# Two-layer recurrent and routed-expert kernel: steps split into parts, a new order of the steps, and fewer pauses on GpSimd

## The reference

```
xn = layernorm(x); x = x + mixer0(xn) * silu(experts0(xn))
xn = layernorm(x); x = x + mixer1(xn) * silu(experts1(xn))

mixer0: xx = shift(xn) - xn; m = tanh((xn + xx*maa_x) @ w1) @ w2      # five token mixes: w, k, v, r, g
        r, k, v, g = from xn + xx*(maa + m); w = decay + tanh(xw @ dw1) @ dw2
        y_t = r_t (S + u k_t v_t);  S = exp(-exp(w_t)) S + k_t v_t     # 2 heads of 64
        out = (groupnorm(y) * silu(g)) @ Wo
experts0: top 2 of 8 by xn @ Wg, softmax of the two; each (silu(x W1) * (x W2)) W3, hidden 256
mixer1: softmax attention, 16 heads of key size 8, over the 512 tokens of a batch
experts1: top 2 of 8, the input of each scaled by a sigmoid gate, plus one shared expert, hidden 256
```

## Time and profile before

| | |
|---|---|
| median of 3 runs (lowest to highest) | 2901.74 us (2898.67 to 2910.47) |
| the profiled execution, its own time | 2902.1 us |
| its span | 2900.3 us, mean granted TensorE clock 0.951 |
| TensorE busy (PE) | 2514.9 us, 87% |
| weight loads (PEld) | 1770.9 us, 61% |
| VectorE busy | 1731.5 us, 60% |
| ScalarE busy | 1411.9 us, 49% |
| GpSimd busy | 1328.8 us, 46% |
| indirect gathers on GpSimd | 256 of 0.99 us, 253.7 us |
| pauses on GpSimd | 192 of 1.68 us, 322.5 us |
| chain that ended last | PE 52%, issue 18%, POOL 15%, ACT 7%, DVE 7% |

### The profile page before, as it was taken

One profiled execution on the slowest core, in us unless ns is written; L12 is line 12 of the kernel. 1 busy time (PEld: TensorE's weight loads), 2 busy tenths in 40 slices (PEclk: granted clock), 3 DMA queues, 4 the chain that ended last, 5 costly groups with the idle time before them and its releaser, 6 DMA issues.

```text
span 2900.3 us, 54969 instructions
## 1 busy us (share of the span) xinstructions
PE 2514.9 (87%) x18122; PEld 1770.9 (61%) x18122; DVE 1731.5 (60%) x4229; ACT 1411.9 (49%) x2613; POOL 1328.8 (46%) x1332
## 2 busy tenths in 40 slices
PE   5678888988889898898989888898898989989887
PEld 2556666666666666566666666666666666666644
DVE  3355657566565755656566565655656666565653
ACT  1234554554545454455545455454454545455545
POOL 2545353555535255443544535355443534535211
PEclk6779999999999999999999999999999999999989
DMA  4233334334333333423334333333424334333222
GB/s 121 69 118 99 114 97 119 114 110 126 96 110 108 112 108 109 125 87 114 113 103 122 94 115 102 118 106 110 125 83 120 116 93 123 100 115 97 79 64 70
DMA packets 384822, 306.26 MB, mean 106 GB/s; under 512 B 37440, under 2 KB 376096, under 8 KB 384544
## 3 DMA queue, kind: packets, MB, share of 16 engines
q1 hardware_dynamic: 368160, 269.16, 31.4%
q0 software_dynamic: 16384, 33.59, 4.0%
HBM read 247.15 MB, written 54.39 MB: 104 GB/s over the span
## 4 chain that ended last, share of the span: by engine, by line
PE 52%; issue 18%; POOL 15%; ACT 7%; DVE 7%; DMA 1%; SPq 0%; another core or an unknown queue 0%; POOLq 0%; ACTq 0%; DVEq 0%
PE bank_st L846 6%; PE bank_s L831 6%; PE bank_y L691 5%; PE bank_g L672 5%; PE bank_pv L860 5%; PE bank_h L672 5%; POOL yg L1137 4%; POOL pause_sb L1061 3%; DVE rowmax L1374 2%; PE bank_mix L702 2%; ACT probs L1010 2%; PE bank_mix L743 2%; ACT ks L995 2%; DVE xn L1245 1%; PE bank_mix L765 1%
## 5 line engine op out<-in xcount | busy, mean ns | idle before, releaser
L1374 DVE TENSOR_REDUCE rowmax<-bank_s 128x1 f32<-128x512 f32 x1016 | 699.2, 688 | 446.1 <-PE bank_s L831 388.6
L1010 ACT ACTIVATE probs<-bank_st 128x512 f32<-128x512 f32 x992 | 589.5, 594 | 373.9 <-PE bank_st L846 350.3
L831 PE MATMUL bank_s<-ks,qs 128*128 128x512 f32 x1016 | 451.5, 444 | 122.1 <-DVE rowmax L1374 118.6
L846 PE MATMUL bank_st<-qs,ks 128*128 128x512 f32 x992 | 501.3, 505 | 47.2 <-ACT probs L1010 45.0
L1061 POOL TENSOR_TENSOR pause_sb<-ones_sb,power_sb 128x8 f32<-128x8 f32 x192 | 322.5, 1680 | 197.4 <-DMA ys_d<-y_sb 102.5
L831 PEld LDWEIGHTS bank_s<-ks,qs 128*128 128x128 f32 x1016 | 196.7, 194 | 219.5 <-DVE rowmax L1374 138.6
L846 PEld LDWEIGHTS bank_st<-qs,ks 128*128 128x128 f32 x992 | 190.7, 192 | 168.1 <-ACT probs L1010 107.9
L691 PEld LDWEIGHTS bank_y<-wbuf,hid 128*128 128x128 f32 x1920 | 254.2, 197 | 60.3 <-DVE hid L1268 26.8
L672 PEld LDWEIGHTS bank_h<-xT_sb,wbuf 128*128 128x128 f32 x1920 | 253.7, 195 | 57.0 <-issue 25.4
L672 PEld LDWEIGHTS bank_g<-xT_sb,wbuf 128*128 128x128 f32 x1920 | 260.9, 199 | 41.8 <-issue 23.3
L672 PE MATMUL bank_h<-xT_sb,wbuf 128*128 128x128 f32 x1920 | 267.4, 282 | 18.0 <-DVE th L1256 17.3
(11 more groups left out here) (244 smaller groups left out, 3874.3 us busy)
## 6 DMA issues: line engine op xcount, KB each, us to landing
wbuf<-up SPq DMA_DIRECT2D x480, 128.0 KB
wbuf<-gate SPq DMA_DIRECT2D x480, 128.0 KB
wbuf<-down SPq DMA_DIRECT2D x480, 128.0 KB
xs_sb<-xs_d SPq DMA_DIRECT2D x96, 256.0 KB
ys_d<-y_sb SPq DMA_DIRECT2D x96, 256.0 KB, 2.5
xs_sb<-xs_d SPq DMA_DIRECT2D x32, 192.0 KB
ys_d<-y_sb SPq DMA_DIRECT2D x32, 192.0 KB, 2.6
x_next<-x SPq DMA_DIRECT2D x16, 256.0 KB, 3.2
```

The lines of the kernel that those rows point to most:

```text
L831: mm(room(s, b)[:], qs[:, slot, q * P:(q + 1) * P], ks[:, slot, j, :], start=True, stop=True).then_inc(filled[b], 1)
L846: mm(room(s, b)[:], ks[:, slot, j, k * P:(k + 1) * P], qs[:, slot, :], start=True, stop=True).then_inc(filled[b], 1)
L1010: A(probs[:, turn % PRING, h % HG, :], ps[:], ACT.Exp).then_inc(emptied[b], 1)
L1374: v.reduce_max(rowmax[:, h // HG % 2, NT * (h % HG) + q:NT * (h % HG) + q + 1], content(s, b)[:], AX).then_inc(emptied[b], 1)
```

## The change

Four steps become several, each with a due time of its own, so that other steps of the same engine can stand between the parts:

- `norm` keeps the moments and `vareps`; the wait for `rstd` and the four `xn` are `normx`.
- `route` keeps the top two; the gates (a softmax or a sigmoid of the two scores, `wtmp`) are `weigh`.
- `rank` keeps the first four of the 15 instructions of `places`; `place` 1, 2 and 3 have the rest.
- `wkv` keeps the group norm's moments and `gvar`; the two `yn` instructions and the wait for GpSimd's power are `yn`.
- the four `ks` copies of `stack` are four steps `keys`, 0.76 us of the plan apart; the wait for a free slot is a function of its own.

No instruction of these is added or removed. The pause of `rest()` stays only ahead of the fourth and seventh DMA of each group of eight, 8 a batch.

All constants of the plan are set anew, and so are the offsets in `LATER` for all five engines. In GpSimd's order the offsets of the kinds that the text below speaks of go from 0.26 to 0.22 (`norm`), 0.28 to 0.28 (`gather`), -0.54 to -0.54 (`decays`), 0.48 to 0.34 (`scatter`); in VectorE's `norm` has -0.06 and `normx` 0.42. The diff without the long `LATER` tables and without the bodies that only move into another branch:

```diff
-PERIOD = 167.91
-MIX_START = 0.91
+PERIOD = 167.87
+MIX_START = 0.94
 MIX_EVERY = 5.92
-DECAYS_BEFORE = 5.86
-CROSS_BEFORE = 5.77
-FINISH_AFTER = 4.27
+DECAYS_BEFORE = 7.76
+CROSS_BEFORE = 3.72
+FINISH_AFTER = 4.9
...
-WEIGHTS_BEFORE = 17.22
-GATHER_AFTER = 8.11
-COMBINE_AFTER = 29.52
-YOUT_AFTER = -0.18
-NORM0_AT = 100.17
+WEIGHTS_BEFORE = 23.74
+GATHER_AFTER = 7.68
+COMBINE_AFTER = 25.79
+YOUT_AFTER = -0.21
+NORM0_AT = 100.28
...
-RANK_AFTER = 4.58
-SCATTER_AFTER = 1.7
-FETCH_AFTER = 7.18
+RANK_AFTER = 4.29
+SCATTER_AFTER = 21.46
+FETCH_AFTER = 1.99
...
-SCATTER_EVERY = 3.18
-GATHER_EVERY = 1.5
-MIX0_EARLY = 16.89
-MIX0_STEP = 0.0
-UNITS0_EARLY = -2.61
-SOFT0_EARLY = 0.0
-UNITS15_EARLY = -19.74
-SOFT15_EARLY = 0.0
-ROUTE15_EARLY = 4.71
-FETCH_BEFORE = 19.53
...
+SCATTER_EVERY = 2.36
+GATHER_EVERY = 2.42
+MIX0_EARLY = 10.13
+MIX0_STEP = -0.03
+UNITS0_EARLY = 0.43
+SOFT0_EARLY = 0.01
+UNITS15_EARLY = 4.52
+SOFT15_EARLY = -0.27
+ROUTE15_EARLY = 0.33
+NORMX_AFTER = 0.73
+WEIGH_AFTER = 2.86
+PLACE_AFTER = 1.82
+YN_AFTER = 1.52
+KEYS_EVERY = 0.76
+FETCH_BEFORE = 17.18
...
+    due[0, "yn"] = due[0, "wkv"] + YN_AFTER
...
+        due[layer, "normx"] = due[layer, "norm"] + NORMX_AFTER
+        due[layer, "weigh"] = due[layer, "route"] + WEIGH_AFTER
         due[layer, "rank"] = due[layer, "route"] + RANK_AFTER
+        for i in (1, 2, 3):
+            due[layer, "place", i] = due[layer, "rank"] + PLACE_AFTER * i
...
+        for j in range(HG):
+            due[1, "keys", g, j] = due[1, "stack", AK, g] + abs(KEYS_EVERY) * j
...
                 elif kind == "stack":
...
                     if which[0] == AQ:
-                        A(qs[:, group % RING, :], ps[:], ACT.Copy).then_inc(emptied[misc], 1)
-                    else:
-                        for j in range(HG):
-                            rows = slice(32 * j, 32 * j + 32)
-                            last = A(ks[rows, group % RING, j, :], ps[rows, :], ACT.Identity, bias=cols_sb[rows, COL_KONE:COL_KONE + 1])
+                        free_slot(n, which[1])
+                        A(qs[:, (NG * n + which[1]) % RING, :], content(s, misc)[:], ACT.Copy).then_inc(emptied[misc], 1)
+                elif kind == "keys":
+                    g, j = which
+                    if j == 0:
+                        free_slot(n, g)
+                    rows = slice(32 * j, 32 * j + 32)
+                    last = A(ks[rows, (NG * n + g) % RING, j, :], content((n, 1, "stack", AK, g), misc)[rows, :], ACT.Identity,
+                             bias=cols_sb[rows, COL_KONE:COL_KONE + 1])
+                    if j == HG - 1:
                         last.then_inc(emptied[misc], 1)
...
             def rest(i):
-                if i % REST == 0:
+                if i > 0 and i % REST == 0:
...
                     row_mean_var(n, src, layer)
+                elif kind == "normx":
+                    src = (x_next, x1[n % 2])[layer]
                     dve.wait_ge(rstd_done[layer], n + 1)
...
+                elif kind == "yn":
+                    wkv, k = (n, 0, "wkv"), NT * NH0
...
                     dve.wait_ge(grstd_done, n + 1)
...
+            def weigh(s):
...
                 dve.wait_ge(gate_exp[layer], n + 1)
```

More of the change, by code:

```diff
@@ L95 @@
[L95 to L97 removed]
+STACK_BEFORE = 8.59
+PV_AFTER = 3.61
+MROW_AFTER = 3.47
+HEADS_AFTER = 2.05
 LAST_AFTER = 5.4
[L99 to L110 removed]
@@ L218, in due @@
             at -= UNITS0_EARLY
-    elif n == 0 and kind in ("stack", "smax", "mrow", "soft", "pv", "headsT"):
+    elif n == 0 and kind in ("stack", "keys", "smax", "mrow", "soft", "pv", "headsT"):
         at -= SOFT0_EARLY
@@ L247, in fills @@
         return [VB] if which[1] == 0 else []
-    if kind in ("keep", "load", "mixed", "norm", "decays", "weights", "yout", "shared", "scatter", "fetch", "gather", "combine"):
+    if kind in ("keep", "load", "mixed", "norm", "decays", "weights", "yout", "shared", "scatter", "fetch", "gather", "combine", "normx", "weigh", "place", "yn", "keys"):
         return []
@@ L1020, in step, with free_slot @@
                     A(headsT_sb[:], content(s, misc)[:], ACT.Copy).then_inc(emptied[misc], 1)
+            def free_slot(n, g):
+                group = NG * n + g
+                if group >= RING:
+                    before = group - RING
+                    old = (before // NG, 1, "soft", HG * (before % NG) + HG - 1, NT - 1)
+                    b = fills(old)[0]
+                    act.wait_ge(filled[b], fill(old, b))
             def decays(n, i):
@@ L1434, in places @@
                 r, pick = ranks[layer], pick_sb[layer]
-                if n >= 2:
-                    dve.wait_ge(gathered[layer], 16 * 2 * NT * (n - 1))
-                    dve.wait_ge(down_done[layer], len(DOWNS[layer]) // B * (n - 1))
+                count, upto_e, start = (nblk[layer][:, i, :] for i in range(3))
+                part = s[3] if s[2] == "place" else 0
                 def flat(a):
                     return a.rearrange("p e q -> p (e q)")
-                v.tensor_copy(r[:], content(s, misc)[:, 0:2 * NT * E].rearrange("p (a q e) -> p a e q", a=2, q=NT)).then_inc(emptied[misc], 1)
@@ L1449, in places @@
-                dve.wait_ge(sig, done + 2)
-                count, upto_e, start = (nblk[layer][:, i, :] for i in range(3))
-                v.reduce_sum(count, over[layer][:], AX).then_inc(sig, 1)
-                dve.wait_ge(sig, done + 4)
-                v.tensor_tensor(place[layer][:], place[layer][:], r[:, 0], ALU.add).then_inc(sig, 1)
-                v.tensor_tensor_scan(upto_e, ones_sb[:].to_broadcast([P, E]), count, 0.0, ALU.mult, ALU.add).then_inc(sig, 1)
-                dve.wait_ge(sig, done + 6)
@@ L1456, in places @@
-                v.tensor_tensor(start, upto_e, count, ALU.subtract).then_inc(sig, 1)
-                v.tensor_tensor(ends[layer][:], numbers_sb[0:1, 0:NB].unsqueeze(2).to_broadcast([1, NB, E]),
-                                upto_e[0:1].unsqueeze(1).to_broadcast([1, NB, E]), ALU.is_ge).then_inc(sig, 1)
-                dve.wait_ge(sig, done + 7)
-                v.scalar_tensor_tensor(out=place[layer][:], in0=start.unsqueeze(2).to_broadcast([P, E, NT]), scalar=float(P), in1=place[layer][:],
-                                       op0=ALU.mult, op1=ALU.add).then_inc(sig, 1)
```

93 lines of the change are left out of this document (55 added, 38 removed).

## The result

The changed kernel takes 2796.7 us, median of four runs (2788.2 to 2798.8), against 2900.4 (2898.7 to 2910.5): a ratio of 0.963 (95% interval 0.960 to 0.966). The prediction was 2809 us, 2775 to 2880. The profiled execution has a span of 2797.0 us, mean granted clock 0.963. I compare by a landmark that comes once a batch, the first `xn` of layer 0. From the fourth to the last of them (12 intervals) the span has 2073.2 us before and 1984.0 after: the cadence fell from 172.8 to 165.3 us, 89 of the 103 us. The third interval gave 7.2 more and the stretch behind the last landmark 11.2; up to the third landmark the kernel became 4.4 us slower. These two ends are of this one execution.

The account below looks back on a forecast made before the run. Bound: TensorE's in-order queue, busy 87% of the span, plus its waits. From 2902.1 us: stall and clock -110, key copies -8, parts 0, new waits +33, start -4, end -4, sum -93, giving 2809 us; range 2775 to 2880.

Parts of the forecast that it names:

- stall and clock together, all batches: At layer 0's norm: TensorE's stalls (56 us) and low clock (12 and 42 us) go, -110 us, bounds 0 to -120.
- `elwc` behind the key copies: On ScalarE: one copy leaves TensorE's 1.6 us wait, -0.5 us x 15 = -8 us, bounds -24 to +10.
- VectorE's other parts: Routing, placing and group norm in pieces on VectorE: value 0, bounds -15 to +10 us.
- new wait for `xmixT`: TensorE waits about 1.3 us a batch for GpSimd's `xmixT`, part of a +33 us term, bounds 0 to +75.
- crosses and `fetch`: 0.5 us a batch each for the crosses and the fetch, added within the +33 us term of new waits.
- start, to the third landmark: First batch: a pause goes (-1.9 us), mix and experts are reordered; -4 us in all, bounds -8 to +8.
- end: Last gathers lose a pause (-1.9 us), last experts' steps stand earlier in the plan; -4 us, bounds -8 to +6.
- The pauses: On GpSimd: 64 of 192 pauses go, 107 us, worth nothing except ahead of `rstd`, at start and end.
- Rival (b): Mixed gathers and scatters on GpSimd hold `xmixT`; slower once TensorE's wait passes 7.3 us, 2930 us at 8; chance 0.08.
- The clock: Sign on TensorE: every 8 us window of a middle batch at 1.00, all intervals alike, near 167 us.
- (a): At the norm: exponentials hold GpSimd, `rstd` at 1109, TensorE still waits some 1.5 us; about 2865 us, chance 0.19.
- (c): At the norm: `normx` directly behind `norm` stalls as before, only pauses go; 2896 us, chance 0.08.

Follow-up runs that it names:

- e4_after_rest3: The changed kernel with the pause ahead of the first DMA of a group back, three a group: 2892.0 us, ratio 0.995 to the kernel before.

## Why the prediction was right

Step by step, per batch where nothing else is said:

| step | predicted | measured |
|---|---|---|
| wait for `rstd` on VectorE | 6.4 to about 2 us | 6.4 to 2.4 |
| stall of TensorE behind it | 3.7 to 0 | 3.7 to 0; all of its `rowmax` waits 7.6 to 2.3 |
| stall and clock together, all batches | -110 us | -100 us (rstd ahead alone) |
| `elwc` behind the key copies | -0.5 | -0.5, but worth nothing in time |
| VectorE's other parts | 0 (-15 to +10 in all) | some -15 in all, in the new order |
| new wait for `xmixT` | +1.3 | +1.2 |
| crosses and `fetch` | +1.0 | not seen |
| cadence | near 167 | 165.3 |
| start, to the third landmark | -4, and a stall less | +4.4, and -1.7 in the second execution |
| end | -4, and a stall less | -11.2, and -1.6 in the second |

**The norm.** The mechanism was right, and its size nearly: the order arithmetic gave `rstd` about 1.0 us behind the end of `vareps`, the trace has 1.3. Two runs show it from both sides, by the move alone (-100 us) and by its reverse (+139 us). That the last interval of before lacked the event was the best evidence for the size, and the run bears it out.

**Where the 12 us between forecast and result lie.** Errors cancel, and that the median is so near is in part luck. The forecast has 85 us in 15 batches, 5.7 each, the trace 7.4 in each of 13: 22 us more. The one us a batch for the crosses and the fetch is not in the trace, and the clock and the other waits gave a little more. For the start and the end the forecast has -19 us with their share of the batches; the trace has -6.8 in one execution and -3.3 in the other. At the start TensorE's idle time is 4 us longer than before in both executions: its transposes of the experts' rows (`bank_mix` L668) wait 9.5 and 10.9 us behind `moved`, up to 8.0 at once, which the kernel before has nothing like, and its wait for layer 1's `xn` is 9.3 and 9.2 us in place of 5.6. These are the steps of batch 0 that I had only bounded. What differs between the two executions is the clock: up to the third landmark 63.1 us of full speed are lost before, 71.7 in the one and 63.1 in the other; behind the last landmark 24.2, 9.9 and 26.8.

**The pauses: the step that was wrong in its words.** The prediction called the removed pauses "worth nothing by itself except ahead of `rstd`", at the start and at the end. In the new order the third pause costs 91 us (2892.0 against 2800.5) when it comes back, and the place is the mixed run of DMAs ahead of `xmixT`. My sum for that run counted three pauses in it and came to 27.2 us (the trace has 25.8) and to an `xmixT` that is just late; with two more of 1.87 us it would have given a wait of several us. The number was in the working, the conclusion on the pauses was not drawn from it. Rival (b) is this mechanism, and it is what e4_after_rest3 runs into.

**The parts.** "Value 0", with the later pieces late by 0.7 us a batch at the worst, missed that a step in pieces ends later and what stands in line behind its end. Alone, the parts cost 45 us. That the layer 0 scatters move 20 us later was read as a matter of margin for their fetch. With them so late GpSimd no longer stands for `index` with the factors of the tree behind it: in the changed kernel the wait of GpSimd for `index` is 2.4 us in all; before it was 61.3 at the pause and 271.9 at `xgate`.

**The clock.** "Every 8 us window of a middle batch has a clock of 1.00 and all intervals are alike" was wrong. The long stretch at 0.50 behind the norm is gone, but short ones remain, and the intervals lie between 162.6 and 166.8 us. The run with `rstd` ahead gave 100 us where the forecast had 110. In its 12 middle intervals the cadence fell by 6.8 us, where the forecast's terms make 7.4. One reason is that not all of the low clock went: of the 54.6 us of full speed lost in these intervals 5.1 stayed. The price that the forecast set on the low clock is borne out. The batches of that run with a clock of 1.00 take 165.5 us, the longer ones of before 174.3; less the stall of 3.7 that leaves 5.0 us for 6.8 us of full speed, against a forecast of 5.2. By the rule of the Trainium skill (TensorE: Matmul & The Clock Gate, "HAM oscillation"), half of a throttled stretch, it would be 6.8, so for this move the rule is too high. Between the kernel before and the changed one waits and clock in full do add up, 4.6 and 2.7 of 7.4 us, so the smaller price is no rule either.

**Rivals.** (a) halfway: no. The exponentials do hold GpSimd, by 2.0 us ahead of gather 0, as the forecast had counted in part, but `rstd` starts 1.3 us behind `vareps` and TensorE has no stall. (b): the wait is there with 1.2 us, far from its 7.3. (c): refuted by the runs with `rstd` moved; pauses alone in the old order gave 32 us, more than its 6, because one of them stood ahead of `rstd`.

## What to carry to other kernels

Look in the waits of an engine off the bottleneck for one that is equally long each time, and follow the releaser's own queue back: here one small instruction stood behind DMAs that had nothing to do with it, and moving it gave 100 of 2900 us. A step cut in pieces ended later here, by some 4 us, so see who waits for its end in order, and whether that can be moved back with it. The price of a filler instruction is to be read in each stretch of its queue in the new order, not off the engine's share of busy time (46% here). And before the start or the end of one trace is explained, look at a second one of the same kernel.

## What the runs showed of the hardware that was not expected

- Sixteen indirect DMAs from GpSimd in a row, each 1.0 us and 0.3 us apart, without the two pauses of 1.7 us among each eight: near their end TensorE stood 1.3 to 3.7 us in each middle batch. The cause is open.
- Behind the stall of 3.7 us the granted clock was below 1.00 in one to three windows of 8 us, down to 0.50. In the changed kernel, whose middle batches have no idle time of TensorE above 1.65 us, it still fell, mostly to 0.79 in one window, about once a batch, at changing places.
- Two executions of the same changed kernel lost 9.9 and 26.8 us of full speed behind the last landmark, and took 386.6 and 396.3 us there.
- The kernel before varied between 2870 and 2917 us over the sets, 1.6%; the changed kernel between 2788 and 2809.
